# An attention and feed-forward block: the product of the sums, its turn and the context's turn moved one step later, and one more tile added up on GpSimd

## The reference, cut to what matters

```
result = embeddings @ w_qkv
scores = einsum('bnqd,bnkd->bnqk', q, k) / sqrt(512)
probs  = softmax(scores, axis=-1)
ctx    = einsum('bnqk,bnkd->bnqd', probs, v)
x      = layernorm(x + out)
```

## Time and profile before

| | |
|---|---|
| median of 3 runs | 3723.65 us (3722.68 to 3725.44) |
| profiled execution | 3722.25 us, span 3720.5 us |
| TensorE busy | 96% of the span |
| VectorE, GpSimd, ScalarE busy | 82%, 67%, 47% |
| chain that ended last | TensorE 70%, VectorE 10%, GpSimd 4% |
| granted TensorE clock, mean | 0.994 |

### The profile page before, as it was taken

How to read it: one execution, slowest core, us unless ns; L and a number is a source line. 1 busy time by engine, 2 the same in 40 slices (tenths; PEclk the granted TensorE clock), 3 DMA queues, 4 the chain that set the end, 5 groups by cost and what they waited for, 6 DMA issues and landing times.

```text
span 3720.5 us, 58214 instructions
## 1 busy us (share of the span) xinstructions
PE 3569.6 (96%) x21226; PEld 1562.3 (42%) x21226; DVE 3035.9 (82%) x4562; ACT 1740.4 (47%) x3072; POOL 2484.8 (67%) x1626
## 2 busy tenths in 40 slices
PE   4799999999999999999999999999999999999898
PEld 2334444334443344343444344433444334444244
DVE  9877898778977789778987789877898778877687
ACT  3466523664246632565236652366424663255522
POOL 2289655885569855797458865588555985569744
PEclk9899999999999999999999999999999999999999
DMA  5211233022321234111431223302232122311022
GB/s 184 89 29 35 69 87 86 18 50 79 93 62 31 45 94 97 45 30 39 113 96 31 41 66 90 86 18 49 75 95 65 29 48 73 73 42 28 1 75 65
DMA packets 412462, 234.55 MB, mean 63 GB/s; under 512 B 331152, under 2 KB 357776, under 8 KB 412048
## 3 DMA queue, kind: packets, MB, share of 16 engines
q1 hardware_dynamic: 412176, 230.82, 24.4%
HBM read 72.09 MB, written 32.24 MB: 28 GB/s over the span
## 4 chain that ended last, share of the span: by engine, by line
PE 70%; DVE 10%; issue 8%; POOL 4%; DMA 1%; ACT 1%; SPq 1%; DVEq 0%; POOLq 0%; ACTq 0%
PE SC L1768 18%; PE CT L1732 9%; PE R L727 7%; PE SC L1717 7%; DVE mx L633 7%; PE R L707 7%; PE R L1768 6%; PE R L1790 6%; PE CT L1790 6%; PE R L739 2%; PE R L717 2%; POOL wd L1293 2%; PE R L749 1%; POOL x L1293 1%; DVE split L627 1%
## 5 line engine op out<-in xcount | busy, mean ns | idle before, releaser
L633 DVE TENSOR_REDUCE mx<-R 128x1 f32<-128x512 f32 x2048 | 1282.5, 682 | 283.7 <-PE R L727 282.3
L1438 ACT ACTIVATE arena<-SC 128x512 f32<-128x512 f32 x1364 | 754.4, 603 | 395.0 <-PE SC L1717 330.5
L1768 PE MATMUL SC<-wgu,split 128*128 128x512 f16 (+1 forms) x3456 | 705.5, 361 | 5.3 <-DMA split<-split 5.3
L1293 POOL TENSOR_TENSOR wd<-wd,arena 128x1024 f32<-128x1024 f32 x216 | 514.5, 2408 | 93.3 <-DVE wd L1574 59.2
L1768 PEld LDWEIGHTS SC<-wgu,split 128*128 128x128 f16 x3456 | 337.4, 98 | 356.1 <-DMA split<-split 7.7
L1438 ACT ACTIVATE wd<-SC 128x512 f32<-128x512 f32 x684 | 385.4, 603 | 204.1 <-PE SC L1717 175.0
L1327 POOL TENSOR_TENSOR arena<-arena,sc_h 128x512 f32<-128x512 bf16 (+2 forms) x144 | 178.0, 1250 | 420.3 <-DVE arena L556 420.3
L707 PE MATMUL R<-xT,wqkv 128*128 128x512 bf16 x1536 | 399.6, 381 | 7.5 <-DVE split L627 6.4
L1481 ACT ACTIVATE arena<-SC,gain 128x512 f32<-128x512 f32 (+1 forms) x192 | 125.0, 651 | 584.0 <-PE R L1768 301.6
L727 PE MATMUL R<-ks_even,qs_even 96*128 96x512 bf16 x1024 | 378.8, 384 | 20.1 <-DVE mx L633 10.2
L727 PE MATMUL R<-arena 96*128 96x512 bf16 x1024 | 381.6, 382 | 8.5 <-DVE split L627 4.1
(11 more groups left out here) (151 smaller groups left out, 5245.8 us busy)
## 6 DMA issues: line engine op xcount, KB each, us to landing
x<-n_L_attn_embeddings_dram SPq DMA_DIRECT2D x72, 256.0 KB, 3.3
wd<-wd_kept SPq DMA_DIRECT2D x32, 512.0 KB, 4.6
out_dram<-x SPq DMA_DIRECT2D x64, 256.0 KB, 2.9
ks_even<-split SPq DMA_DIRECT2D x192, 64.0 KB, 2.0
qs_even<-split SPq DMA_DIRECT2D x384, 32.0 KB, 1.9
arena<-split SPq DMA_DIRECT2D x192, 64.0 KB, 2.0
arena<-split SPq DMA_DIRECT2D x384, 32.0 KB, 1.9
arena<-n_L_attn_embeddings_dram SPq DMA_DIRECT2D x48, 256.0 KB, 3.8
```

The costliest lines, as they stand in the source:

```text
L633: nc.vector.reduce_max(mx[:, j:j + 1], ring_of(ring, job)[:, :], AX_X).then_inc(max_done, 1)
L1293: nc.gpsimd.tensor_tensor(acc[u % 2][i], acc[u % 2][i], probs_of(s)[:, hs, :], ALU.add).then_inc(pool_sum, 1)
L1438: nc.scalar.activation(probs_of(s)[:, hd, :], SC[e % SLOTS][:, :], ACT.Exp, scale=SCALE).then_inc(exp_done, 1)
L1768: last = nc.tensor.matmul(GU[kk % 2][which][:, 0:w], xhT[i % 2][:, part_x * KH + k, :], wgu[:, part_w * KH + k, which * I + first:which * ...
```

## The change

In units 2 to 6 of each batch the product of the sums of the unit before goes from step 2 to step 3, its transposition from step 3 to step 4, and the context's transposition from step 4 to step 5. Units 1 and 7 stay as they are. In unit 5 of batches 1 to 7 GpSimd adds tile 7 as well (two more instructions), and the product of unit 5's sums, made in unit 6, no longer reads that tile (8 instructions fewer).

```diff
 def pool_sums(u):
-    return POOL_SUMS[u % UNITS] - (1 if u >= UNITS and u % UNITS in (UNITS - 3, UNITS - 2) else 0)
+    return POOL_SUMS[u % UNITS] - (1 if u >= UNITS and u % UNITS == UNITS - 2 else 0)
...
     ends = u == UNITS - 1
+    late = 1 if 1 < u < UNITS - 1 else 0
...
     if u > 0:
-        other += [("sumT", u - 1, 0)] if t == SUM_T_STEP else []
-        other += [("ctx", u - 1, 0)] if t == (CTX_STEP_LAST if ends else CTX_STEP) else []
+        other += [("sumT", u - 1, 0)] if t == SUM_T_STEP + late else []
+        other += [("ctx", u - 1, 0)] if t == (CTX_STEP_LAST if ends else CTX_STEP + late) else []
...
-    total = [("sum", u - 1, 0)] if u > 0 and t == SUM_STEP else []
+    total = [("sum", u - 1, 0)] if u > 0 and t == SUM_STEP + late else []
```

## The result

The changed kernel takes 3736.73 us (median of 6 runs, 3733.41 to 3739.44), the kernel before 3722.22 us on the same chip (6 runs, 3720.63 to 3725.44): ratio 1.0038, 95% interval 1.0027 to 1.0048. It is 14.5 us slower. The profiled execution took 3735.0 us with a span of 3733.2, 12.75 us more than before. The forecast was 3729 us within 3714 to 3738, and "no change" was its largest chance; the time lies in the range, near its end, and the loss (0.38%) is beyond the 0.2% from which on the prediction called a kernel slower.

What follows compares the result with a forecast made beforehand. TensorE, busy for 96% of the span, was taken to bound the kernel. About +6 us in batches 1 to 6, 0 in batch 0 and -0.7 in batch 7 gave +5.3 us, a median of 3729 us, range 3714 to 3738.

Steps and rivals of the forecast that it cites:

- no change: Whole kernel: time not told apart from the kernel before, within about 0.2% or 7.4 us; chance 0.59.
- Unit 3: Unit 3: wait for GpSimd's last addition goes, step 5 wait shrinks; -0.67 us in each of 8 batches, -5.4 us.
- the stall of step 5: Unit 3, projection waiting for its ring slot: the context's transposition fills part; of some 0.97 us about 0.66 remain.
- Units 2 and 4: Units 2 and 4: lone product costs 0.2 us, slot waits shrink; -0.1 us, 16 times, bounds +0.2 and -0.4.
- The product's way in and out: Step 3, product without a weighing: pays both changes of shape, about 0.2 us; 0.31 after its maximum, 0.95 to the next.
- Unit 5: Unit 5: VectorE sets the pace, context falls amid its backlog; +0.2 us, bounds 0 and +0.6, batch 0 +0.4.
- Unit 6, the collision: Unit 6: GpSimd's tile 7 additions and VectorE's first sums exclude each other on SBUF; +1.7 us in batches 1 to 6.
- batch 7: Batch 7, unit 6: clock partly lower, saved work worth double, collision costs the same; 0 us, bounds -3 and +2.
- The add of the context: GpSimd's add waits for a context done 3.5 to 4 us later; cost 0, up to 0.6 us on GpSimd.
- ScalarE's copy: Step 3: copy of the product comes late, TensorE waits 0.4 us in some 24 units; +10 us, 3739, chance 0.13.
- a fall of the clock: TensorE's clock falling in other stretches: named as a sign that the prediction is wrong, no size given.
- The first rival: Unit 6: VectorE's first sums escape GpSimd's second tile 7 addition, gaining 0.4 us instead of losing 1.7; 3714, chance 0.17.

Runs made afterwards that it cites:

- the third run: The changed kernel, but GpSimd leaves tile 2 out of the sums in unit 5 of batches 1 to 7: 3720.32 us.

## Why the prediction was right or wrong

**Unit 3** (forecast -0.67): -0.59. The steps are as forecast: no wait for GpSimd, and the stall of step 5 shorter by 0.30 us (0.81 to 0.51 in the rows) where 0.31 was reckoned (0.97 to 0.66).

**Units 2 and 4** (-0.1 each): -0.04 and -0.03. The product's way in and out is near the forecast (0.31 and 1.00 us, where 0.31 and 0.95 were named), and the lengths of the units show that it is covered.

**Unit 5** (+0.2, batch 0 +0.4): +0.3, and +0.9 in batch 0. The sign was right, batch 0 was undersized.

**Unit 6, the collision** (+1.7): +1.64 at the full clock. The two engines exclude each other as argued from one case; this is shown by the first sum of 3.18 us, which fell to 1.22 when GpSimd was done earlier, and unit 6 lost its extra length with it. The rule of the Trainium skill (SBUF — State Buffer, Who interferes with whom) held also in its other half: a maximum, whose input is in PSUM, took 0.69 us beside GpSimd's additions. In batch 7 unit 6 came out 1.1 us shorter (forecast 0, bounds -3 and +2).

**The add of the context** (0): in unit 6 of batch 2 GpSimd sat idle 0.1 us ahead of it. Right.

**ScalarE's copy** (rival, +10 us): it cost nothing, but by a hair. The prediction called it a sign of being wrong if this copy released the last maximum of step 3, and in units 2 and 4 of all eight batches it does. In batch 2 unit 4, where the product begins at 1206.10 (ScalarE, then TensorE's weight load for that maximum):

```profile
1207.24 0.60 ACT L1401 ACTIVATE wd<-R 128x512 f32<-128x512 f32 x1 [0.65 <-PE R L740]
...
1207.88 0.10 PEld L728 LDWEIGHTS R<-ks_even,qs_even 96*128 96x128 bf16 x1 [0.24 <-ACT wd L1401]
```

The copy ends 1.74 us behind the product's start (forecast 1.8), and the load waits 0.24 us for it. The maximum itself starts at 1207.98, 0.21 us behind the score before it, which is the usual step, so TensorE's matmuls lose nothing. The rival's times were right to 0.1 us; the 0.4 us more of lateness that it needed didn't come.

**The sum** is where it failed. By its own terms the measured units give -0.59 - 0.07 + 0.30 + 1.64 = +1.28 in each of batches 1 to 6, +7.7; +0.4 in batch 0 (-0.58 - 0.08 + 0.91 + 0.18); -1.4 in batch 7 (-0.57 - 0.07 + 0.29 - 1.07): +6.7 against the forecast +5.3. Two terms were priced at nothing. The standstill of 1.7 us that the collision makes takes TensorE's clock down, 1.44 us in 2 batches of the profiled run: +2.9; the prediction named a fall of the clock only as something that would make it wrong. And the waits for transfers, +4.0, for which the prediction had no term; that they follow TensorE's instructions is shown by two runs for the part at the transposed rows (7.4 against 4.6 us, 8.3 against 4.9; the 0.8 us in batch 7 excepted), while the other 1.0 us was not traced. 6.7 + 2.9 + 4.0 = 13.6, where 12.75 were measured; of the rest, the attention part of batch 0 begins 1.7 us earlier (173.0 us before, 171.3 after), and single waits make up the remainder; neither was traced.

So the direction and the main mechanism were right, and the largest chance, "no change", was put on the wrong side of the bound, because 5.3 us were held where 12.75 came (14.5 by the medians). That 3736.73 lies in the range is partly luck: the upper part of the range was made of the bounds of units 2, 4, 5 and batch 7 and of the rival with the copy, and those stayed near their middle or cost nothing; what filled it were the clock and the transfers, which no part of the range stood for.

**The first rival** (first sums slip through, 3714): it didn't happen, but its price for unit 6 was about right, as the third run had it at -0.30 where -0.4 was named (that run took 3720.32 and not 3714, with the waits for transfers still in it). One sentence of it was wrong: "whichever goes first, the other of the pair comes between the two first sums". With the sums one maximum earlier the first sum was issued under GpSimd's first addition, and both of GpSimd's additions went ahead of it. Whether a GpSimd instruction gets in between two of VectorE's sums that follow each other at once was not tried.

## What to carry to other kernels

When work goes to GpSimd, ask what VectorE instruction with two SBUF inputs falls due in the idle stretch that is filled, and count its delay as the time until GpSimd's queue next has a gap, not until its present instruction ends. Price a new standstill of TensorE with the lower clock behind it as well: after 1.7 us of standstill that was 1.44 us more here, in some batches and not in others. A change of several units should be cut by unit first: here one unit held the gain and one the loss, and two runs told them apart.

## What the runs showed of the hardware that had not been expected

- A VectorE sum that waits for GpSimd doesn't get in between two GpSimd instructions that follow each other at once. Its end was 1.08 us past the second addition both when it was issued during that one (3.18 us) and when it was issued during the first (3.79 us), and 1.09 past the context's add where that came last. The same section of the Trainium skill says that the order of issue decides who blocks; here GpSimd kept VectorE out over its next instruction too, though that one was issued later than VectorE's.
- After the same 1.7 us of standstill in unit 6 the granted clock fell in some batches and not in others: of batches 1 to 6 in two with the change and in two with the sums one maximum later, in three with units 5 and 6 alone, in four with the context's add behind tile 7 and in four with the product taken twice (there and with units 5 and 6 alone the standstill of batch 2 was shorter, 1.43 and 1.58 us). With 1.9 to 2.1 us (the sums one maximum earlier) it fell in four. With a standstill of about 3 us (the tile alone) it fell in all six; without one (before, units 2 to 4 alone, tile 2 out) in none.
- The same holds for TensorE's wait for the transposed rows ahead of the feed-forward part of batch 5. It was 1.9 to 2.6 us in the eight kernels with the short product, and the granted clock was 0.5 right behind it in three of them (2.24 us with tile 2 out, 2.02 with the context's add behind tile 7, 2.60 with the sums one maximum later), but not with the change (2.47).
- 16 instructions fewer per batch in TensorE's queue (batches 1 to 7) moved TensorE's wait for the transposed rows from 4.6 to 5.8 us up to 6.9 to 8.9, and to other batches, with the same transfers.
